# Layer 1's last two weight pieces behind the first tiles, SP reading all tiles, and large buffers at multiples of 512 bytes

## What is computed

```python
e = jnp.stack([tbl_f[ids[:, f]] for f in range(39)], axis=1)    # 512 x 39 x 16
x0 = xk = e
for W in (f0, f1, f2):
    z = jnp.einsum('bfd,bgd->bfgd', x0, xk).reshape(b, f * g, d)
    xk = jnp.einsum('bpd,pm->bmd', z, W)                        # m = 128
    outs.append(xk)
z = jnp.sum(jnp.concatenate(outs, axis=1), axis=-1)             # 512 x 384
h = jnp.concatenate([z, dense_ctx], axis=1)
h = jnp.maximum(h @ W_top1 + b_top1, 0.0)
h = jnp.maximum(h @ W_top2 + b_top2, 0.0)
y = h @ W_top3
```

## Time and profile before

| | us |
|---|---|
| median of three runs | 661.05 |
| the profiled execution | 660.73 |
| its span | 658.5 |
| PE busy | 625.5 |
| DVE busy | 522.7 |
| POOL busy | 502.3 |
| ACT busy | 341.3 |

### The profile page before, as it was taken

The page is one execution under the profiler, slowest core; times in us unless marked ns, Lnnn a source line. Parts: engine busy times, 40 slices in busy tenths (PEclk is TensorE's granted clock), DMA queues, the critical chain, the costliest instruction groups (busy, mean ns, idle before and its releaser), DMA issues.

```text
span 658.5 us, 10966 instructions
## 1 busy us (share of the span) xinstructions
PE 625.5 (95%) x3110; PEld 470.4 (71%) x3110; DVE 522.7 (79%) x1655; ACT 341.3 (52%) x1152; POOL 502.3 (76%) x486
## 2 busy tenths in 40 slices
PE   0559999999999999999999999999999999999998
PEld 0237777777788777777788777777788777778873
DVE  4239988989985888989984888989984889988911
ACT  3224555646463565646463564646463564646612
POOL 6717888989894889989894888989894897657620
PEclk9969999999999999999999999999999999999999
DMA  7423405641320404031220404131230403000000
GB/s 226 106 57 111 127 3 134 236 105 32 68 68 2 132 3 121 15 90 47 60 75 3 131 4 110 25 92 44 52 84 2 131 4 104 27 1 2 0 1 0
DMA packets 59014, 43.40 MB, mean 66 GB/s; under 512 B 37648, under 2 KB 42926, under 8 KB 58826
## 3 DMA queue, kind: packets, MB, share of 16 engines
q1 hardware_dynamic: 52334, 37.52, 19.6%
q0 software_dynamic: 5120, 1.32, 2.9%
q10 hardware_dynamic: 1500, 3.87, 1.7%
HBM read 40.75 MB, written 1.94 MB: 65 GB/s over the span
## 4 chain that ended last, share of the span: by engine, by line
PE 91%; another core or an unknown queue 3%; DVE 2%; DMA 2%; ACT 1%; issue 1%; ACTq 1%; DVEq 0%
PE strip L816 22%; PE strip L820 22%; PE strip L817 22%; PE acc L776 14%; PE acc L847 4%; PE strip L834 3%; PE strip L847 1%; DVE scaled L593 1%; DMA g_sum<-in_L_rec_f 1%; PE strip L918 1%; PE acc L785 1%; ACT w_hi L717 1%; ACTq L720 1%; PE strip L896 0%
## 5 line engine op out<-in xcount | busy, mean ns | idle before, releaser
L593 DVE SCALAR_TENSOR_TENSOR scaled<-strip,x_t,scaled 128x128 f32<-128x128 f32 x1216 | 331.5, 340 | 31.0 <-PE strip L820 29.5
L816 PE MATMUL strip<-w_hi,x_hi 128*128 128x512 f32 (+1 forms) x640 | 297.0, 464 | 3.4 <-ACT x_hi L646 3.4
L820 PE MATMUL strip<-w_hi,x_lo 128*128 128x512 f32 (+1 forms) x640 | 249.4, 390 | 0.0
L817 PE MATMUL strip<-w_lo,x_hi 128*128 128x512 f32 (+1 forms) x640 | 248.8, 389 | 0.0
L488 POOL TENSOR_TENSOR added<-added,product 128x512 f32<-128x512 f32 x128 | 173.0, 1351 | 83.4 <-ACT product L702 76.9
L702 ACT ACTIVATE product<-strip,x_t 128x128 f32<-128x128 f32 x512 | 147.0, 373 | 126.5 <-PE strip L820 113.2
L478 POOL DMA_INDIRECT found<-in_tables,rows x160 | 159.6, 998 | 28.4 <-issue 11.2
L816 PEld LDWEIGHTS strip<-w_hi,x_hi 128*128 128x128 f32 x640 | 120.5, 188 | 52.5 <-issue 18.8
L817 PEld LDWEIGHTS strip<-w_lo,x_hi 128*128 128x128 f32 x640 | 120.8, 189 | 45.5 <-issue 25.3
L820 PEld LDWEIGHTS strip<-w_hi,x_lo 128*128 128x128 f32 x640 | 120.3, 188 | 25.8
L776 PE MATMUL acc<-z,w 117*128 117x512 f32 (+1 forms) x238 | 116.5, 572 | 9.1 <-issue 9.1
(11 more groups left out here) (57 smaller groups left out, 190.2 us busy)
## 6 DMA issues: line engine op xcount, KB each, us to landing
shifted<-x_fields SPq DMA_DIRECT2D x105, 234.0 KB
x_thrice<-x_fields SPq DMA_DIRECT2D x15, 234.0 KB
found<-in_tables,rows POOLq DMA_INDIRECT x160
w<-in_L_rec_f SPq DMA_DIRECT2D x1, 2496.0 KB, 11.9
g_sum<-in_L_rec_f ACTq DMA_DIRECT2D x4, 512.0 KB
shifted<-x_half_fields SPq DMA_DIRECT2D x10, 117.0 KB
x_once<-x_fields SPq DMA_DIRECT2D x15, 78.0 KB
x_fields<-found SPq DMA_DIRECT2D x15, 72.0 KB
```

What stands on the lines that cost most here:

```text
L593: dve.scalar_tensor_tensor(into, strip[:, slot_of_strip(q) % Y_BANKS, j, :], x0_t[:, c % 2, s, f:f + 1], onto, ALU.mult, ALU.add).then_inc ...
L816: pe.matmul(into, x1_hi[:, c % 2, columns], hi, start=True, stop=False)
L817: pe.matmul(into, x1_hi[:, c % 2, columns], lo, start=False, stop=False)
L820: pe.matmul(into, x1_lo[:, c % 2, columns], hi, start=False, stop=True).then_inc(strip_ready, 1)
```

## The change

Four things are changed.

- Layer 1's pieces 0 to 2 are loaded and split as before (`W1_EARLY = 3`). ACT issues pieces 3 and 4 only when tile 5 of part 0 has landed (`shifted_in[T0 - 2]`), and splits them after `x1_hi` of part 0; DVE makes their `w1_lo` after `x1_lo` and the sum of part 0.
- SP reads all seven tiles of part 0; ACT reads none. ACT moves out the dense products before it issues the late pieces.
- POOL issues the five gathers of the first half before it computes the row numbers of the other chunks (it issued one). PE starts the dense products (L861) when the first half has been gathered, and no longer when it has been written.
- The buffers are declared in another order, behind a spare one of 384 bytes a partition. In the built program every large buffer then starts at a multiple of 512 bytes; the small ones and those of odd size come last.

```diff
+W1_EARLY = 3
...
+        sb("spare", [P, 3 * P // 4])
         ident = sb("ident", [P, P])
-        mask = sb("mask", [P, TILE_B])
         w0 = sb("w0", [ROWS, T0, MAPS])
...
-        ids = sb("ids_sb", [P, CHUNKS + 2, GATHERS], I32)
-        rows = sb("rows", [P, CHUNKS, GATHERS], I32)
-        found = sb("found", [P, E_SLOTS, GATHERS, D])
...
-        x0_t = sb("x0_t", [P, 2, SUBS, FIELDS])
-        x0_diag = sb("x0_diag", [P, SUBS, TILE_B, FG])
...
+        mask = sb("mask", [P, TILE_B])
+
+        ids = sb("ids_sb", [P, CHUNKS + 2, GATHERS], I32)
+        rows = sb("rows", [P, CHUNKS, GATHERS], I32)
+        found = sb("found", [P, E_SLOTS, GATHERS, D])
+        x0_t = sb("x0_t", [P, 2, SUBS, FIELDS])
+        x0_diag = sb("x0_diag", [P, SUBS, TILE_B, FG])
...
-                for t in range(T0 if i else T0_BY_SP):
+                for t in range(T0):
...
-            gather(0)
+            for n in range(HALF_GATHERS):
+                gather(n)
             add_first_rows(1, CHUNKS, CHUNKS)
             pool.wait_ge(rows_ready, 2)
-            for n in range(1, AHEAD):
+            for n in range(HALF_GATHERS, AHEAD):
                 gather(n)
...
-            for i in range(W1_PIECES - 1):
+            for i in range(W1_EARLY):
                 low_w1(i)
             for t in range(T0):
                 products0(0, t)
-            low_w1(W1_PIECES - 1)
             low_x1(0)
             sum_x1(0)
+            for i in range(W1_EARLY, W1_PIECES):
+                low_w1(i)
...
+            for i in range(W1_EARLY):
+                load_w1(i)
             act.wait_ge(dense_turned, 1)
             act.wait_ge(dense_zeroed, 2)
             act.copy(dense_t[0:D, :], dense_bank).then_inc(dense_kept, 1)
-            for i in range(W1_PIECES):
-                act.wait_ge(w1_in[i], 16)
-                act.copy(w1_hi[:, w1_fields(i), :], w1_raw[:, w1_fields(i), :]).then_inc(w1_hi_ready, 1)
-            act.wait_ge(written_half[0], 16 * WRITES)
-            for t in range(T0_BY_SP, T0):
-                act.dma_start(shifted[0:ROWS, t, columns_of(0)],
-                              shifted_fields(0, PER_TILE * t, PER_TILE, 1)).then_inc(shifted_in[t], 16)
+            for i in range(W1_EARLY):
+                high_w1(i)
...
+            act.wait_ge(shifted_in[T0 - 2], 16)
+            for i in range(W1_EARLY, W1_PIECES):
+                load_w1(i)
             keep_x0_t(0)
             high_x1(0)
+            for i in range(W1_EARLY, W1_PIECES):
+                high_w1(i)
...
-            pe.wait_ge(written_half[0], 16 * WRITES)
+            pe.wait_ge(gathered_half[0], 16 * HALF_GATHERS)
```

More of the change, by code:

```diff
@@ L24 @@
 T0 = -(-SHIFTS // PER_TILE)
-T0_BY_SP = 3
 ROWS = PER_TILE * FIELDS
@@ L234, in build_program @@
         out2 = sb("out2", [MAPS, BATCH])
-        dense = sb("dense_sb", [P, QUARTERS, D])
         dense_t = sb("dense_t", [P, BATCH])
-        bias1 = sb("bias1", [P, H1 // P])
-        bias2 = sb("bias2", [P, H2 // P])
         wt1 = sb("wt1", [P, 3, H1])
@@ L243, in build_program @@
         wt2 = sb("wt2", [P, H1 // P, H2])
+        mask = sb("mask", [P, TILE_B])
[4 more added lines that the diff above has]
+        x0_diag = sb("x0_diag", [P, SUBS, TILE_B, FG])
+        dense = sb("dense_sb", [P, QUARTERS, D])
+        bias1 = sb("bias1", [P, H1 // P])
+        bias2 = sb("bias2", [P, H2 // P])
         wt3 = sb("wt3", [P, H2 // P])
@@ L709, in _, with load_w1, high_w1 @@
             act.dma_start(w0_mirror, a["w0_lower"]).then_inc(w0_in, 16)
-            for i in range(W1_PIECES):
+            def load_w1(i):
                 act.dma_start(w1_raw[:, w1_fields(i), :], a["L0_rec_f1"][:, w1_fields(i), :]).then_inc(w1_in[i], 16)
+            def high_w1(i):
+                act.wait_ge(w1_in[i], 16)
+                act.copy(w1_hi[:, w1_fields(i), :], w1_raw[:, w1_fields(i), :]).then_inc(w1_hi_ready, 1)
+            for i in range(W1_EARLY):
+                load_w1(i)
             act.wait_ge(dense_turned, 1)
```

## The result

The change takes 658.02 us (median of five runs, 656.11 to 659.16) where the kernel before, in the same comparison, takes 661.32 (660.89 to 662.85): ratio 0.9948, interval 0.9928 to 0.9967. That is 3.3 us faster, not 12. The profiled execution took 657.83 us, with a span of 656.0.

A forecast was written before the change was run, and what follows sets the result against it. PE was taken as the bound, busy 625.5 of 658.5 us, with its start paid in full. A 12 us gain at the start and 0 for addresses gave 648.7, less 0.3 below the median: 649.0 us, range 617 to 659.

The forecast's parts named there:

- The direction: Whole kernel: faster by over 0.2%, chance 0.87.
- A: Forecast case: waits before tiles 5 and 6 go with ACT's tile queue, no matmul changes; 645 to 653 us, chance 0.42.
- rival B: Start: the waits aren't the tiles'; PE's signals arrive late, part of the 12 us stays; 653 to 659, chance 0.23.
- The first half: Gathering and writing part 0's first half: 2.2 us earlier, between 0 and 2.6; SP writes at 12.9.
- Tiles: Part 0's tile reads, all by SP: last product at 25.9, long waits gone, strip 0 at about 28 us.
- Late pieces: Layer 1's last two weight pieces: all w1_lo at 32.4 us, ACT's first product at 32.5 instead of 44.15.
- What follows part 0: Part 1's writing and tiles after the start: some tenths lost, within 0.35 us.
- The gain of 12: Start: total gain 12 us, between 11.65 (ACT's first product earlier) and 14.4 (strip 0 earlier).
- Addresses: Main-stage float32r matmuls with moved buffers: gain taken as 0, between 0 and 33 us, or a few us lost.
- Rival C: Main stage: addresses hold float32r matmuls back; up to 33 us from PE, DVE then near; 617 to 636, chance 0.22.
- Slower (D): Start: lateness is the tile's transfer, so strip 0 comes 2 us later than before; 663 us, chance 0.07.

The follow-up runs named there:

- sp_all: The kernel before with SP reading all seven tiles of part 0, nothing else changed: 660.83 us beside 661.28 for the kernel before, ratio 0.9992.
- before_hold15: The kernel before with POOL's first gather row parted: gathers from 15 on wait for x1_hi of part 0. 657.36 us beside 660.87, ratio 0.9945.
- early5: The changed kernel with all five weight pieces loaded and split early: 644.89 us beside 646.92 for the kernel before, ratio 0.9967.
- after_d: The changed kernel as it is, timed again on a chip where the kernel before takes 646.93 us: 646.58 us, ratio 0.9994.
- addr_new: The kernel before with only the new order of the buffers: 660.08 us beside 661.28, ratio 0.9979.
- addr_old: The changed kernel with buffers declared in the old order, without the spare one: 648.98 us beside 646.92 for the kernel before, ratio 1.0034.
- after_hold15: The changed kernel with POOL's first gather row parted: gathers from 15 on wait for x1_hi of part 0. 651.53 us beside 660.87, ratio 0.9874.
- after_c: The changed kernel as it is, timed again on a chip where the kernel before takes 660.73 us: 657.79 us, ratio 0.9947.
- pool_hold_b: The changed kernel with POOL's gathers from 10 on held until x1_hi of part 0 is ready: 658.69 us beside 660.73, one run.
- the three of hold15: before_hold15, after_hold15 and the latter with all five weight pieces loaded at the start: 657.36, 651.53 and 654.75 us beside 660.87.

## Why the prediction was wrong

**The direction** was right, and the time, 658.02, lies in the range, near its end of 659. The likeliest case, A, was not what happened; rival B was, down to its argument that ACT's copy was late in the earlier trace rows though it waits for no tile.

**The first half** was right: SP wrote at 13.10 (12.9 predicted), `x0_thrice` was issued at 15.81.

**Tiles.** The issue and the last product were right (25.45 for 25.9). The step that failed is this one's half-sentence, "what would bring the gain is that the long waits are gone": it took them for waits for ACT's tiles. I had about 12 us of unexplained waits in the trace and put them on the part that the change takes away. sp_all, which takes away just that part, gains 0.45 us, with an interval that holds no change at all; before_hold15, which leaves it and parts the gathers, moves strip 0 by 13.6 us. The waits are for increments of PE that come late while POOL issues a long row of gathers, on some chips. The change leaves the row as long as it was, so they only moved: 6.3 us onto `x1_hi`, 4.7 onto ACT's first product. Strip 0 at 33.55 instead of 28 is the first of them, and the first product at 41.21 instead of 32.5 both.

**Late pieces.** Their size was right: on the punctual chips ACT's first product came at 31.5 to 31.7, for 32.5. What I missed is that this is a loss once the lateness is out of the way: with all pieces early it comes at 30.26, and the kernel takes 1.7 us less (early5 beside after_d). I had counted ACT's two roundings as lying "in the 11.65", which compares with a start that was itself disturbed.

**What follows part 0.** I allowed 0.35 us. PE waited 5.5 us for DVE's `z` of part 1; that is ACT's late first product again. But the term was too small without lateness too: in after_d, on a punctual chip, PE waits 1.6 us for `x_once` of part 1 and another 1.6 in two waits for DVE's `z`. How much of this the change brought isn't known, for want of a trace of the kernel before there.

**The gain of 12.** With strip 0 14.4 and the product 11.65 earlier, I took a value between. On the late chip they were 8.9 and 2.9, and the whole gain was 3.3: it went by ACT's first product, the smaller of the two. In the eleven traces of kernels with no hold and an unparted row, strip 40 starts 37.1 to 39.3 us behind ACT's first product, but anything from 38.9 to 46.9 behind strip 0. That the seven banks let PE run no further ahead is the likely reason, and not shown by itself. Of those 3.3 us addr_new puts 1.2 on the addresses, which leaves some 2.1 for the start.

**Addresses.** I took 0, between 0 and 33. A float32r matmul is faster by 3.6 ns, not by 18, and the kernel by 1.2 us on a late chip and 2.4 on the punctual ones. Rival C had the mechanism in small: DVE is near, PE has 2.3 us of gaps, and most of the 6.0 us is given back. Which of the moved buffers matters was not tried apart. The 215.7 ns of the Trainium skill ("TensorE: Matmul & The Clock Gate", section "Wait — 56ns, not 53.3ns?") were reached by no float32r matmul in either layout; its 16-byte lines ("SBUF — State Buffer", section "Specifications (TRN2)") predict no difference between two layouts that are both at multiples of 32 bytes, and the trace shows 232.7 and 229.1 ns.

**Slower (D)** did not occur: no tile came later than I took, and PE's increments at 31.60 and 37.19 in the first trace already spoke against it. (Its added lateness is 13.4 us, 16.9 less 3.5, and not 14.4; the 663 doesn't rest on it.) Where a part of the change was slower, in addr_old, it was for the most part by the late pieces (1.7 of 2.06 us) and not by a transfer.

What stays open: why signals are late on some chips and not on others, how many gathers it takes (the idle time of the new waits begins five to eight gathers into a second row of eleven), and what holds PE's increments between the matmul's end and the semaphore. Of versions, after_hold15 is the best on a late chip (0.9874) and early5 on a punctual one (0.9967); after_hold15 was not run on a punctual chip.

## What to carry to other kernels

A wait whose releaser the profile calls remote or issue, with the work that it waited for long done, must not be booked to the part that a change removes. See first whether the trace has the increments of the semaphores that it waits for: the one just ahead of its start tells whose signal it was. Look for one more waiter of another engine that is late in the same stretch, ask what all of them share, and hold that back in one run before anything is built on it. A gain at the start is worth what the last of the engines that start there gains, here ACT's first product and not PE's first strip, and only if no longer wait follows (before_hold15 had its first product 14.3 us earlier and gained 3.5); and a start tuned on one chip should be timed on a second, since the very stage that it shortens may be one that other chips don't have.

## What the runs showed of the hardware

- Chips differ by 14 us (2.2%) on the kernel before and by 11 on the change, at a granted clock of 1.00 over the main stage. In the change, which has traces on both kinds, nearly all of it lies in the first 80 us: strip 40 starts at 80.47 us in the first profile and at 69.65 in after_d, while strips 40 to 639 take 543.98 and 543.55.
- On the late chips PE's semaphore increments come up to 9.7 us late while POOL issues gathers one after another every 1.25 us (after_c: recorded at 41.47, the matmul ended at 31.76), and for 3 to 5 us after the row; those of DVE and ACT come on time in the same stretch. Behind 60 us, where POOL issues its gathers one at a time between other work, a few of PE's are still up to 1.2 us late on late chips, and none over 0.15 on punctual ones.
- With POOL held after gather 9 (pool_hold_b) or 14 (the three of hold15), ACT sees the end of layer 0 within 0.04 us, and the lateness comes back some gathers into the next row.
- Moving the large buffers to multiples of 512 bytes shortens the float32r matmuls of 512 columns that stream their weights from there from 232.7 to 229.1 ns. Those of 384 columns changed unevenly: 176.0 to 172.0 ns for hi by hi, 172.5 to 174.9 for hi by lo.
